# A selective state-space decoder layer on one core: state matmuls ahead of the transposes, out-projection three slots behind, parameters in a buffer of their own

## The chip, the core and the metric

The kernel runs on one core of a Trainium2 chip. The metric is the device time of one execution in microseconds (us); smaller is better. The kernel before took 816.22 us, the median of three runs (814.41 to 816.71).

## The reference, cut to what matters

Two sequences of 256 tokens (512 tokens, 512 features) go through three layers: a Mamba-2 style layer, a product with a quantised context, and a small feed-forward layer with a low-rank mixture. Nearly all time goes to the first:

```
h     = rmsnorm(layernorm(x)) * norm_w
gate, hidden, B, C, dt = split(h @ in_proj_w.T)       # 8192, 8192, 1024, 1024, 128
hidden, B, C = silu(causal_conv4(hidden, B, C))
M     = (C B^T) * exp(segment sums of A*dt)            # per head, lower triangle
y     = M @ (hidden * dt) + D * hidden
y     = groupnorm(y * silu(gate)) * gnorm_w            # 8 groups of 1024 channels
x     = x + h_in + y @ out_proj_w.T
```

There are 128 heads of 64 channels. The kernel takes two heads (128 channels) at a time, a *pair*: 64 pairs, 8 in each of 8 groups. B and C, and the norm of y, belong to a group.

## The kernel before, in words

Work is written out by hand for each engine, in program order, with semaphores between them. Every engine runs the same loop of 64 *slots* (`slots`, L200 to 209): slot s, with k = s mod 8 its place in group g. The first and the last group are written out, the six between are a hardware loop. Matrix weights and activations are split into an upper and a lower part (`_hi`, `_lo`), so a projection is three passes of four matmuls of 128x128 by 512 columns (`project`, L1093): 12 matmuls.

- **TensorE, slot s** (`@block.tensor`, `slot`): `project` of the hidden channels of pair s into `ps_h`; `scan_heads` (L1183), 8 matmuls issued as 16, which multiply the masked decay matrix of pair s-1 by its `hid_dt` into `ps_y`; at k = 0 the products of B and C (L1141, L1142) into `ps_z` and `ps_t`, at k = 1 the channel sums of the group before (L1204) into `ps_t`; `project` of the gates into `ps_z`; `project_out` (L1196, 12 matmuls) of pair s-2 into `ps_out`, which collects a group; the four transposes of `hidT` of pair s into `ps_t` (L1066). At k = 6 and 7 the projections of B and of C of the next group follow, into `ps_z`.
- **VectorE**: `hid_dt` from `ps_t` (L835, pair s-1), at k = 2 the four additions of the finished group to `acc` (`add_group`, L876), the convolution of pair s in three steps (`conv`, L728), `v` and `yg` (`combine`, L846 and L852, pair s-1), the masking of the decay of pair s (L792), `y_lo` (L858).
- **ScalarE**: the first tap of the convolution (`tap`, L477), `hidT` (L539), the gate (L545), `y_hi` and `sq` (`finish_y`, L561 and L567, pair s-1), and the 8 exponentials of the decay of pair s+1 (`decays`, L531). It loads a function table before the exponentials and another before `hidT`.
- **GpSimd**, for pair s+1: copies of its own sums (L329), split of the input weights (L288), split of the output weights (L292), lower part of the input weights (L297), the triangle of `csx` (L337), lower part of the output weights (L302); at k = 4 the split of the B and C weights (L379, L307); then the sum of squares (L399). At k = 1 it also takes the root for the group's norm (L385). It starts a slot when `project_out` of pair s-3 is done.
- **SyncE's queue**, for pair s: the row of weights and parameters (L237, after `y_lo` of pair s-4), two loads of `csx` (L245, after `decays` of pair s-2), at k = 1 the B and C weights of the next group (L259, after the Silu of the present C).

Buffers: `w_raw` and the output weights have 4 places; input weights, `csx`, `decay`, `hidT`, `gate`, `yg`, `sq` have 2; `ps_h`, `ps_z`, `ps_y`, `ps_t` one PSUM bank each.

The wait between the transposes and `scan_heads` of the next slot is what sets the order around the change:

```
eng.wait_ge(dve_hiddt, s)      # scan_heads of slot s, pair s-1
eng.wait_ge(dve_m, s)
```

## Time and profile before

| what | value |
|---|---|
| median of 3 runs | 816.22 us |
| the profiled execution | 814.25 us |
| its span, first to last instruction | 812.4 us |
| mean granted TensorE clock | 0.996 |
| TensorE busy | 787.0 us (97%) |
| VectorE, ScalarE, GpSimd busy | 615.7, 603.5, 624.1 us |
| moved by DMA | 94.93 MB, mean 117 GB/s |

The 1.85 us between span and time lie ahead of the first and behind the last instruction. The end of a matmul is modelled, so neighbours overlap in the record: the pace of matmuls is read from one start to the next, and the idle time given before a matmul is a little shorter than the time lost.

### The profile page before, as it was taken

Reading aid. Unit: us, or ns where it says so; the run is one execution under the profiler, and the core shown is the slowest. Engines: PE = TensorE matmul, PEld = TensorE weight load, DVE = VectorE, ACT = ScalarE, POOL = GpSimd, SP = SyncE. Lnnn points to the kernel's source line nnn. Section 1 sums busy time; section 2 is a strip of 40 time slices with the busy share of each in tenths; the row PEclk is TensorE's granted clock in tenths of the full one; section 3 lists DMA queues with packets and bytes.
Section 4 is the critical chain, followed back from the end, with each engine's and each line's share of the span. In section 5 each row is a group of like instructions: output and inputs, shape, how many; then the busy total and the mean of one; then the engine's idle time right before and its main releaser. Section 6 shows DMA issues by size and latency. Waiting matters only on the chain.

```text
span 812.4 us, 13296 instructions
## 1 busy us (share of the span) xinstructions
PE 787.0 (97%) x4322; PEld 607.8 (75%) x4322; DVE 615.7 (76%) x752; ACT 603.5 (74%) x1052; POOL 624.1 (77%) x552
## 2 busy tenths in 40 slices
PE   8798999999999999999999999999999999999897
PEld 7576777777777777777777777777777777777664
DVE  6889978786776867786776867776786867798864
ACT  5788777877788776877688886878688876888442
POOL 6689985799578985799578985799578986798231
PEclk9999999999999999999999999999999999999999
DMA  8452425333243324334233424333233424340001
GB/s 332 146 142 86 130 67 177 122 118 130 92 134 123 129 65 158 127 129 129 91 129 129 129 65 156 129 129 129 91 129 129 129 66 157 130 126 30 4 2 52
DMA packets 48812, 94.93 MB, mean 117 GB/s; under 512 B 3952, under 2 KB 36848, under 8 KB 48784
## 3 DMA queue, kind: packets, MB, share of 16 engines
q1 hardware_dynamic: 48496, 94.06, 35.0%
q10 hardware_dynamic: 288, 0.52, 0.2%
q8 instruction: 15, 0.25, 0.1%
q14 instruction: 13, 0.11, 0.0%
HBM read 93.26 MB, written 1.31 MB: 116 GB/s over the span
## 4 chain that ended last, share of the span: by engine, by line
PE 58%; DVE 21%; ACT 11%; issue 8%; POOL 1%; DMA 0%; ACTq 0%; DVEq 0%
PE ps_z L1093 17%; PE ps_out L1196 14%; PE ps_h L1093 12%; PE ps_y L1183 6%; DVE conv L728 5%; DVE conv_bc L728 4%; ACT decay L531 4%; DVE yg L852 2%; PE ps_t L1066 2%; ACT L531 2%; DVE v L846 2%; ACT conv L477 2%; DVE y_lo L858 2%; DVE decay L792 1%; ACT conv_bc L461 1%
## 5 line engine op out<-in xcount | busy, mean ns | idle before, releaser
L728 DVE SCALAR_TENSOR_TENSOR conv<-ps_h,w_raw,conv 128x510 f32<-128x510 f32 (+2 forms) x192 | 143.2, 746 | 94.5 <-ACT conv L477 90.0
L531 ACT ACTIVATE decay<-csx,cs_own 128x256 f32<-128x256 f32 (+1 forms) x512 | 184.4, 443 | 1.0
L297 POOL TENSOR_TENSOR win_lo<-w_raw,win_hi 128x1024 fp32r<-128x1024 f32 x64 | 153.4, 2397 | 0.5 <-DMA csx<-cs_rows 0.5
L399 POOL TENSOR_TENSOR sqacc<-sqacc,sq 128x512 f32<-128x512 f32 x47 | 70.3, 1496 | 94.1 <-ACT sq L567 94.1
L792 DVE TENSOR_TENSOR decay<-decay,cbm 128x1536 f32<-128x1536 f32 x64 | 126.0, 1968 | 2.4 <-ACT decay L531 2.4
L539 ACT ACTIVATE hidT<-conv 128x512 f32<-128x512 f32 x64 | 40.5, 634 | 94.8 <-DVE conv L728 94.8
L1183 PE MATMUL ps_y<-decay,hid_dt 128*64 128x256 f32 (+1 forms) x1024 | 97.5, 333 | 9.4 <-DVE hid_dt L835 9.4
L337 POOL TENSOR_SCALAR_AFFINE_SELECT csx<-csx 128x512 f32<-128x512 f32 x128 | 105.8, 851 | 0.2 <-DMA csx<-cs_rows 0.2
L1183 PEld LDWEIGHTS ps_y<-decay,hid_dt 128*64 128x64 f32 x1024 | 63.4, 136 | 51.9 <-issue 17.3
L1196 PE MATMUL ps_out<-wout_hi,y_lo 128*128 128x512 f32 x252 | 99.9, 397 | 0.0
L1196 PE MATMUL ps_out<-wout_lo,y_hi 128*128 128x512 f32 x252 | 99.5, 395 | 0.0
L1196 PE MATMUL ps_out<-wout_hi,y_hi 128*128 128x512 f32 x252 | 99.4, 395 | 0.0
L302 POOL TENSOR_TENSOR wout_lo<-w_raw,wout_hi 128x512 fp32r<-128x512 f32 x64 | 94.1, 1470 | 0.1
L858 DVE SCALAR_TENSOR_TENSOR y_lo<-yg,w_raw,y_hi 128x512 fp32r<-128x512 f32 x64 | 92.7, 1448 | 1.6 <-ACT y_hi L561 1.6
L531 ACT ACT_TABLE_LOAD x63 | 80.8, 1283 | 1.2
L1093 PE MATMUL ps_z<-hT_hi,win_hi 128*128 128x512 f32 x256 | 77.1, 423 | 0.5 <-DVE conv_bc L728 0.3
L1093 PE MATMUL ps_h<-hT_hi,win_hi 128*128 128x512 f32 x256 | 73.5, 408 | 0.0
L1093 PE MATMUL ps_z<-hT_lo,win_hi 128*128 128x512 f32 x256 | 70.6, 397 | 0.0
L1093 PE MATMUL ps_h<-hT_lo,win_hi 128*128 128x512 f32 x256 | 70.2, 396 | 0.0
L1093 PE MATMUL ps_z<-hT_hi,win_lo 128*128 128x512 f32 x256 | 69.9, 394 | 0.0
L1093 PE MATMUL ps_h<-hT_hi,win_lo 128*128 128x512 f32 x256 | 69.3, 392 | 0.0
L288 POOL TENSOR_SCALAR win_hi<-w_raw 128x1024 fp32r<-128x1024 f32 x63 | 65.7, 1043 | 0.0
(316 smaller groups left out, 1483.0 us busy)
## 6 DMA issues: line engine op xcount, KB each, us to landing
w_raw<-in_wmain SPq DMA_DIRECT2D x64, 772.0 KB, 4.3
csx<-cs_rows SPq DMA_DIRECT2D x128, 256.0 KB, 3.5
bc_raw<-in_wbc SPq DMA_DIRECT2D x8, 517.0 KB, 3.5
ctx_raw<-in_ctx SPq DMA_DIRECT2D x1, 2048.0 KB, 16.4
bc_raw<-in_wffn SPq DMA_DIRECT2D x2, 512.0 KB, 4.0
out_x<-acc SPq DMA_DIRECT2D x4, 256.0 KB, 2.1
acc<-in_x ACTq DMA_DIRECT2D x2, 256.0 KB, 3.7
acc<-in_x SPq DMA_DIRECT2D x2, 256.0 KB, 3.5
```

The costliest lines, as they stand in the source:

```text
L288: eng.tensor_scalar(win_hi[:, r2, :], w_raw[:, r4, 0:W_IN], 1.0, 0.0, ALU.mult, ALU.add).then_inc(hi_win, 1)
L297: eng.tensor_tensor(win_lo[:, r2, :], w_raw[:, r4, 0:W_IN], win_hi[:, r2, :].bitcast(f32), ALU.subtract).then_inc(low_win, 1)
L302: eng.tensor_tensor(wout_lo[:, r4, :], w_raw[:, r4, W_IN:W_ALL], wout_hi[:, r4, :].bitcast(f32), ALU.subtract).then_inc(low_wout, 1)
L337: eng.affine_select(out=blocks[:, :, to:to + P], in_=blocks[:, :, at:at + P], compare_op=ALU.is_ge, fill=never, base=0, pattern=[[0, 2 * B ...
L399: eng.tensor_tensor(sqacc[:], sqacc[:], sq[:, (k - 1) % 2, :], ALU.add).then_inc(pool_sq, 1)
L531: done = eng.activation(decay[:, r2, b, h, lo:lo + n], csx[:, r2, b, h, lo:lo + n], ACT.Exp, bias=cs_own[:, r2, t, h:h + 1])
L728: eng.scalar_tensor_tensor(out=out_b[:, :, back:], in0=src_b[:, :, 0:S - back], scalar=w[:, TAPS - 1 - back:TAPS - back], in1=out_b[:, :, ...
L792: eng.tensor_tensor(decay[:, r2], decay[:, r2], cbm[:].unsqueeze(2).broadcast_to([P, B, 2, MJ]), ALU.mult).then_inc(dve_m, 1)
L858: eng.scalar_tensor_tensor(out=y_lo[:, q2, :], in0=yg[:, q2, :], scalar=w_raw[:, q4, W_ALL + 6:W_ALL + 7], in1=y_hi[:, q2, :].bitcast(f32) ...
L1093: last = mm(out, w[:, k * P:(k + 1) * P], h[:, k, :], start=n == 0, stop=n == 3 * KT - 1)
L1183: done = mm(ps_y[h * HD:(h + 1) * HD, (b + 1) * S - n:(b + 1) * S], hid_dt[:, q2, src, h * HD:(h + 1) * HD], decay[:, q2, b, h, lo:lo + n] ...
L1196: done = mm(ps_out[:, t, :], y[:, q2, t * P:(t + 1) * P], w[:, q4, :], start=pair == 0 and n == 0, stop=pair == PPG - 1 and n == 2)
```

## The change

1. TensorE's slot runs hidden projection, gate projection, `project_out`, `scan_heads`, transposes. In slots k = 0 and k = 7 `project_out` stands ahead of the gate projection. The products of B and C (k = 0) use `ps_h` in place of `ps_z` and stand ahead of `scan_heads`, and the channel sums move to k = 2.
2. `project_out` takes pair s-3; two of them follow the loop. `combine`, `finish_y` and `lower_y` take pair s-2, the masking pair s-1, `decays` pair s at the start of ScalarE's slot.
3. VectorE's slot runs `combine`, `hid_dt`, additions (k = 3), masking, convolutions, `y_lo`.
4. The eight parameters of a channel leave `w_raw` for `par`, eight places of their own, loaded by a DMA of their own (64 DMAs of 4 KB), so `w_raw` is freed by the lower output weights. 
5. GpSimd starts a slot when the gate projection of pair s-1 is done, splits the output weights of pair s, not s+1, at its slot's end, and does the B and C weights last. `sq` has three places.
6. The load of B and C weights is issued at k = 3.

```diff
@@ SyncE
+                    if late(s - 7):
+                        eng.wait_ge(dve_ylo, s - 7)
+                    eng.dma_start(par[:, k, :], wpar_d[s]).then_inc(w_in[r], 16)
                     if late(s - 3):
-                        eng.wait_ge(dve_ylo, s - 3)
+                        eng.wait_ge(low_wout, s - 3)
                     eng.dma_start(w_raw[:, r, :], wmain_d[s]).then_inc(w_in[r], 16)
...
-                if k == 1:
+                if k == 3:
                     eng.wait_ge(act_bc, 2 * g + 2)
@@ GpSimd slot
-                    eng.wait_ge(w_in[n4], 16 * (2 * g + (k + 1) // 4 + 1))
-                    if first and 0 < k < 3:
+                    eng.wait_ge(w_in[n4], 32 * (2 * g + (k + 1) // 4 + 1))
+                    if late(s):
                         eng.wait_ge(pe_gate, s)
-                    if late(s - 2):
-                        eng.wait_ge(pe_out, s - 2)
...
                     split_in(n4, (k + 1) % 2)
-                    split_out(n4)
                     eng.wait_ge(csx_in[1 - r2], 32 * (4 * g + (k + 1) // 2 + 1))
                     lower_in(n4, (k + 1) % 2, s + 2)
                     select(1 - r2)
-                    lower_out(n4, s + 2)
+                if late(s - 3):
+                    eng.wait_ge(pe_out, s - 3)
+                if k == 3 and not first:
+                    eng.wait_ge(dve_ms, g)
+                    eng.tensor_tensor(rstd[:], ms[:], half_neg[:], ALU.pow).then_inc(pool_rstd, 1)
+                sum_squares(s, g, k, first)
+                split_out(r4)
+                lower_out(r4, s + 1)
                 if k == 4:
                     eng.tensor_scalar(wbc_hi[:], bc_raw[:, 0:BC_W], 1.0, 0.0, ALU.mult, ALU.add).then_inc(hi_wbc, 1)
                     lower_bc(g + 2)
@@ ScalarE slot, its new order (the first two slots have no finish_y)
+                decays(s, k)
+                if k == PPG - 1 and not last:
+                    tap_bc(0, g + 1, ps_z, conv_bc[:])
                 if k == 0:
                     tap_bc(1, g, ps_z, conv_bc[:])
...
+                tap(s, g, k)
+                finish_y(s, g, k, first)
...
                 hidden(s, k)
                 gates(s, k)
-                finish_y(s, g, k, first)
-                if not (last and k == PPG - 1):
-                    decays(s + 1, k + 1)
@@ VectorE slot
+                if not (first and k < 2):
+                    combine(s, k)
                 if not (first and k == 0):
                     scale_hidden(s, k)
...
-                if k == 2 and not first:
+                if k == 3 and not first:
                     add_group(g - 1)
+                if not (first and k == 0):
+                    mask(s, g, k)
                 if k == PPG - 1 and not last:
                     conv_group(0, g + 1, ps_z, conv_bc[:])
...
+                conv_hidden(s, k)
+                if not (first and k < 2):
+                    lower_y(s, k)
@@ TensorE slot
+                turned = k == 0 or k == PPG - 1 and not last
                 eng.wait_ge(low_win, s + 1)
                 if late(3 * s):
                     eng.wait_ge(dve_conv, 3 * s)
+                if k == 1:
+                    eng.wait_ge(dve_cb, 2 * g + 1)
                 project(ps_h[:], win_hi[:, r2, 0:KT * P], win_lo[:, r2, 0:KT * P], pe_hid)
                 if first and k == 0:
                     start_up()
+                if turned and not (first and k == 0):
+                    project_out(s, g, k)
+                if late(s):
+                    eng.wait_ge(act_gate, s)
...
+                project(ps_z[:], win_hi[:, r2, KT * P:], win_lo[:, r2, KT * P:], pe_gate)
+                if not turned and not (first and k < 3):
+                    project_out(s, g, k)
+                if k == 0:
+                    products_of_bc(s, g)
+                if k == 2 and not first:
+                    sum_channels(s, g - 1)
                 if not (first and k == 0):
                     scan_heads(s, k)
...
                 for t in range(TT):
                     done = tr(ps_t[:, t * P:(t + 1) * P], hidT[:, r2, t * P:(t + 1) * P])
...
             def project_out(s, g, k):
-                pair, q2, q4 = (k - 2) % PPG, (k - 2) % 2, (k - 2) % 4
-                eng.wait_ge(dve_ylo, s - 1)
+                pair, q2, q4 = (k - 3) % PPG, (k - 3) % 2, (k - 3) % 4
+                eng.wait_ge(dve_ylo, s - 2)
...
             slots(eng, slot)
+            project_out(PAIRS, GROUPS, 0)
             scan_heads(PAIRS, 0)
-            project_out(PAIRS, GROUPS, 0)
+            eng.wait_ge(low_wout, PAIRS - 1)
+            project_out(PAIRS + 1, GROUPS, 1)
```

## Rows read from the trace of the kernel before

**Rows 1.** The page: busy time of each engine and its share.

```profile
PE 787.0 (97%) x4322; PEld 607.8 (75%) x4322; DVE 615.7 (76%) x752; ACT 603.5 (74%) x1052; POOL 624.1 (77%) x552
```

**Rows 2.** Waits of TensorE, whole span: us in total, times, longest.

```profile
PE ps_y L1183 <- DVE hid_dt L835: 9.4, 13, 2.5
```

**Rows 3.** Busy time in stretches: length, PE, PEld, DVE, ACT, POOL, clock, DMA.

```profile
31.64:65.11 33.47, 30.32 (x160) 23.03 (x158) 27.19 (x36) 28.84 (x56) 26.20 (x22) 0.95 0.44 124
65.11:128.36 63.25, 59.64 (x315) 46.14 (x314) 55.90 (x58) 48.62 (x85) 52.36 (x43) 1.00 0.34 113
334.44:344.89 10.45, 10.45 (x60) 8.06 (x57) 6.70 (x8) 8.58 (x16) 8.25 (x9) 1.00 0.37 126
355.34:366.18 10.84, 10.52 (x60) 8.08 (x58) 10.06 (x9) 8.56 (x16) 10.84 (x8) 1.00 0.36 121
344.89:404.75 59.86, 59.48 (x316) 46.13 (x314) 44.26 (x48) 44.62 (x80) 49.73 (x43) 1.00 0.36 119
723.99:734.99 11.00, 10.51 (x59) 8.07 (x58) 10.76 (x11) 7.55 (x16) 11.00 (x9) 1.00 0.47 167
```

**Rows 4.** The timeline of TensorE in a plain slot (start, us, instructions).

```profile
337.38 1.52 PE L1183 MATMUL ps_y<-decay,hid_dt 128*64 128x256 f32 x16
338.84 1.19 PE L1093 MATMUL ps_z<-hT_hi,win_hi 128*128 128x512 f32 x4
339.86 1.10 PE L1093 MATMUL ps_z<-hT_lo,win_hi 128*128 128x512 f32 x4
340.80 1.09 PE L1093 MATMUL ps_z<-hT_hi,win_lo 128*128 128x512 f32 x4
...
344.54 0.60 PE L1066 MATMUL ps_t<-ident,hidT 128*128 128x128 f32 x4
344.89 0.48 PE L1093 MATMUL ps_h<-hT_hi,win_hi 128*128 128x512 f32 x1
```

**Rows 5.** The same for k = 1, where the channel sums follow the state matmuls.

```profile
317.02 1.05 PE L1204 MATMUL ps_t<-ones,sqacc 128*128 128x1 f32 x8
317.94 0.71 PE L1093 MATMUL ps_z<-hT_hi,win_hi 128*128 128x512 f32 x2
```

**Rows 6.** The timeline of VectorE: the plain slot, then k = 4, 5 and 2.

```profile
342.11 1.75 DVE L792 TENSOR_TENSOR decay<-decay,cbm 128x1536 f32<-128x1536 f32 x1
343.77 0.74 DVE L858 SCALAR_TENSOR_TENSOR y_lo<-yg,w_raw,y_hi 128x512 fp32r<-128x512 f32 x1
...
444.77 2.59 DVE L792 TENSOR_TENSOR decay<-decay,cbm 128x1536 f32<-128x1536 f32 x1
447.28 2.88 DVE L858 SCALAR_TENSOR_TENSOR y_lo<-yg,w_raw,y_hi 128x512 fp32r<-128x512 f32 x1
...
451.34 2.31 DVE L728 SCALAR_TENSOR_TENSOR conv<-ps_h,w_raw,conv 128x510 f32<-128x510 f32 x3 [0.58 <-ACT conv L477]
...
454.44 1.50 DVE L852 TENSOR_TENSOR yg<-v,gate 128x512 f32<-128x512 f32 x1
...
417.11 2.72 DVE L876 SCALAR_TENSOR_TENSOR acc<-ps_out,rstd,acc 128x512 f32<-128x512 f32 x4
```

**Rows 7.** The timeline of GpSimd at k = 4 and 5.

```profile
445.83 3.78 POOL L307 TENSOR_TENSOR wbc_lo<-bc_raw,wbc_hi 128x1024 fp32r<-128x1024 f32 x1
...
453.00 2.39 POOL L297 TENSOR_TENSOR win_lo<-w_raw,win_hi 128x1024 fp32r<-128x1024 f32 x1
```

**Rows 8.** The timeline of ScalarE: a plain slot, then the first group's second slot.

```profile
334.52 2.88 ACT L531 ACTIVATE decay<-csx,cs_own 128x256 f32<-128x256 f32 x8
...
43.21 0.60 ACT L545 ACTIVATE gate<-ps_z 128x512 f32<-128x512 f32 x1 [2.30 <-PE ps_z L1093]
```

**Rows 9.** The timeline of TensorE behind the last slot.

```profile
755.65 0.60 PE L1066 MATMUL ps_t<-ident,hidT 128*128 128x128 f32 x4
757.75 1.52 PE L1183 MATMUL ps_y<-decay,hid_dt 128*64 128x256 f32 x16 [1.50 <-DVE hid_dt L835]
```

**Rows 10.** DMA issues: KB each, median us to landing.

```profile
csx<-cs_rows SPq DMA_DIRECT2D x128, 256.0 KB, 3.5
```

More of the change, by code:

```diff
@@ L19 @@
 N_PAR = 8
-W_ROW = W_ALL + N_PAR
 BC_W = 2 * KT * P
@@ L499, in slot @@
                     decays(s, k)
-                    tap(s + 1, g, k + 1)
-                    decays(s + 1, k + 1)
                     return
+                if first and k == 1:
+                    tap(s, g, k)
+                    decays(s, k)
+                    scale_context(0)
+                    hidden(s, k)
+                    gates(s, k)
+                    return
+                decays(s, k)
+                if k == PPG - 1 and not last:
+                    tap_bc(0, g + 1, ps_z, conv_bc[:])
                 if k == 0:
                     tap_bc(1, g, ps_z, conv_bc[:])
-                    silu_bc(1, g, conv_bc[:])
-                if k == PPG - 1 and not last:
-                    tap_bc(0, g + 1, ps_z, conv_bc[:])
-                    silu_bc(0, g + 1, conv_bc[:])
-                if not (first and k == 1):
-                    tap(s, g, k)
+                tap(s, g, k)
+                finish_y(s, g, k, first)
                 if first:
@@ L514, in slot @@
                     scale_context(PPG - 1)
+                if k == PPG - 1 and not last:
+                    silu_bc(0, g + 1, conv_bc[:])
+                if k == 0:
+                    silu_bc(1, g, conv_bc[:])
                 hidden(s, k)
                 gates(s, k)
-                finish_y(s, g, k, first)
-                if not (last and k == PPG - 1):
-                    decays(s + 1, k + 1)
             def decays(s, k):
@@ L1159, in slot @@
                     eng.wait_ge(dve_cb, 2 * g + 2)
-                if k == 1 and not first:
+                if k == 2 and not first:
                     eng.wait_ge(dve_ms, g)
```

194 lines of the change are left out of this document (94 added, 100 removed).

## The prediction

> **What bounds the kernel now.** I read four views, in this order. The page's busy times put TensorE at 787.0 of 812.4 us [rows 1], so at most some 25 us of plain idle time are to be had by order alone. The waits of TensorE then say that nearly all of what can be named in the loop is one wait: the state matmuls wait for `hid_dt`, 9.4 us in 13 waits [rows 2]. The busy times by stretch show where [rows 3]: a plain slot of the hardware loop lasts 10.45 us and TensorE is busy in all of it, while VectorE has 6.70, ScalarE 8.58 and GpSimd 8.25 us of work. The slot k = 5 lasts 10.84 us. Five slots (k = 4 to the next k = 0) take 59.86 us in the loop, but 63.25 us in the first group. Last, the engines' timelines say what each block costs and what its neighbours are. So the kernel is bound by TensorE's own stream, and the change can give back only waits; no matmul goes away.
>
> **Why the wait exists.** Transposes of pair s-1 close a slot, `hid_dt` follows on VectorE, and the state matmuls come only one hidden projection (12 matmuls, 2.9 us) later. Where VectorE is late, TensorE waits. In the new order the gate projection (2.8 us), `project_out` (2.8 us) and the state matmuls' own turn lie between: 12 matmuls at the pace of 0.94 us for four [rows 4] are 2.8 us, so `hid_dt` and the mask have 8.4 us from the slot's start, not 2.9.
>
> **The sum, against the profiled execution's 814.25 us** (span 812.4).
>
> 1. *Loop, k = 5.* At k = 4 GpSimd has the B and C weights as well and holds up the next slot: 10.84 against 10.45, 0.39 us, in six groups 2.3 us; in the last group 11.00 against 10.45 [rows 3], 0.6 us. In all **-2.9 us**. The new cover: the weights of pair s+1 are split from the gate projection of pair s-1 on, about 4.7 us ahead of slot s, and are needed at its end, 10 us later. B and C cost GpSimd some 3.5 us (the 2.39 us of their shape [rows 7] and about 1.1 for the upper part), so all of it is hidden.
> 2. *First group from its k = 4 on.* 63.25 - 59.86 = 3.4 us above the loop's pace [rows 3], which itself holds the 0.39 us of k = 5: 3.8 us of waits. VectorE is busy 55.90 of the 63.25 us there, since it quantises the context too. That load stays; the slack grows. I take 2.8 of the 3.8 back: **-2.8 us**.
> 3. *Start.* From the second slot to k = 4 takes 33.47 us [rows 3] for three blocks of `project_out`; the new kernel does two in it and owes one (2.8 us) to the end. In the second slot the gate had waited 2.30 us for its projection [rows 8], which now stands right behind the hidden one. I followed the new order by hand with the durations of rows 4, 6 and 8: transposes of the second slot about 41 us, the third slot bound by ScalarE (a table load, 2.88 us of exponentials, the tap, two more, the context's scaling, a table load, `hidT`), k = 4 starting about 61.2 us in place of 65.11. That is 3.9 less 2.8: **-1.1 us**. B and C wait about 1 us longer in the first slot (the convolution of the hidden channels now stands ahead of that of C); this is in the 61.2.
> 4. *End.* Behind the last slot the state matmuls started 2.10 us after the transposes began [rows 9], which themselves take 0.35 us [rows 4]. The `project_out` that is now there (2.8 us) fills these 1.75 us: **-1.7 us**.
> 5. *Changing between blocks.* The state matmuls use weights of 64 columns, all others 128. The step into them keeps a 128-column neighbour before it, so it costs the same. Out of them the gate projection's first four matmuls took 1.02 us against 0.94 for the next four [rows 4]; that goes, since the gate projection follows the hidden one. The transposes follow the state matmuls instead. They took 0.35 us for four [rows 4]; the channel sums, the nearest thing that follows the state matmuls with fresh 128-column weights each time, took 0.92 us for eight [rows 5], 0.115 each, so 0.46 for four. Bounds for each of some 62 slots: -0.08 (transposes at 0.35) and +0.11 (all of it, nothing saved), -5 to +7 us. I take the middle of the two rows, +0.02 each: **+1.0 us**.
> 6. *Additions of the group, k = 3.* Their 2.72 us [rows 6] now stand ahead of the mask and of the convolution of the same slot, whose `hidT` the transposes want 10.05 us after the slot's start. From the slot's start, VectorE ends `hid_dt` at about 2, the additions at 4.7 to 5.3, the mask at 6.4 to 7.2, the convolution (2.31) at 8.7 to 9.5, `hidT` at 9.4 to 10.1. Between nothing and 0.3 us late; seven times: **+1.0 us**.
> 7. *Costed at nothing.* Channel sums, now at k = 2, and B-C products only change place on TensorE; the first has the state matmuls behind it to cover the mean that the transposes wait for (0.15 us of work), the second finds B and C done some 1.5 us early. The 64 parameter loads: one more issue on SyncE's queue per slot, waiting for `y_lo` of seven slots ago; queued behind it are the weights and `csx`, and both now wait for earlier events than before. `csx` is issued after the exponentials of the slot two back and lands 3.5 us later [rows 10], about when GpSimd asks for it; if late it costs GpSimd tenths of the 2 us it idles in a slot. The B and C load at k = 3 waits for a Silu long done, 12 us ahead of its use. Cover for all: GpSimd's slack; without it 3.5 us a group.
>
> Sum: -2.9 - 2.8 - 1.1 - 1.7 + 1.0 + 1.0 = -6.5 us: 807.7 us for the execution profiled, which stands 2.0 us under the median shown. For the median: 816.2 - 6.5 = **809.7 us**.
>
> **A lock between VectorE and GpSimd.** `y_lo` took 0.74 us in the plain slot, but 2.88 us when it met GpSimd's lower part of B and C: it ended at 450.16, 0.55 us after that operation (449.61). The mask before it took 2.59 in place of 1.75 us, and GpSimd's operation 3.78 us, where one of the same shape took 2.39. `yg` took 1.50 us and ended at 455.94, 0.55 us after GpSimd's operation of 453.00 [rows 6, 7]. `v`, `conv` and `hid_dt`, with an operand in PSUM, keep their time (conv 2.31 us beside it). So `yg`, the mask and `y_lo`, and each operation of GpSimd, take turns. Work that must take turns in a slot of 10.45 us: GpSimd's 8.25 us [rows 3] less about 0.1 us at the head of each of its eight operations (its 2.39 us operation ended 2.25 us after the mask let go), 7.4 us; VectorE's 0.55 + 1.6 + 0.55, 2.7 us; together 10.1. Until now GpSimd rested while VectorE did these three, because it waited for `sq`; now it will not.
>
> The Trainium skill, "SBUF — State Buffer", its summary of ports, speaks against this change: a VectorE instruction with two SBUF inputs and a GpSimd instruction that reads SBUF share a port under an exclusive lock, and the later one blocks fully. The trace agrees (twice 0.55 us behind the end of GpSimd's operation). By this rule at its worst the time would be that of the first rival, by VectorE's 6.70 us of the plain slot alone that of the forecast.
>
> **Rivals.**
> - *The lock makes VectorE the bound (slower).* At its worst rows VectorE's slot is v and its wait 0.9, `yg` 1.50, `hid_dt` 0.7, mask 2.59, conv 2.31, `y_lo` 2.88 [rows 6], 10.9 us. It decides where this passes 10.45. In five slots a group, eight groups: 40 x 0.45 = 18 us: 809.7 + 18, less some 5 us where longer slots (k = 0, 1, 6, 7) take up the lag: about 822 us. Against it: all three must meet the longest operation in every slot, and in my schedule one does (about 10.1 us in all). Chance 0.09.
> - *The additions and the first group stay late (no change).* If the group's root is 1 us late behind the lock, k = 3 loses 1.3 us, seven times 9 us, where I have 1; and items 2 and 3 bring nothing: about 815 to 819. For it: the root shares GpSimd with everything else. Chance 0.11.
> - *The first group alone brings nothing.* Items 2 and 3 fail: TensorE's clock was at half for about 3 us after the idle stretch of the second slot (mean 0.95 in the first stretch [rows 3]), and the new third slot idles too. 813 us. Chance 0.12.
> - *Leaving the state matmuls is free.* Item 5 at its lower bound and item 6 at nothing: 802 to 803 us. Chance 0.10.
> - *My forecast*: 805 to 813 us. Chance 0.58.
>
> 0.3% is 2.4 us, about what a measurement can tell from no change. Faster by more: the forecast, the last two rivals, 0.80; within: 0.11; slower: 0.09. The range takes in all but the slow rival and the upper half of the second: 802 to 817.
>
> **What would show it.** Right: no wait for `hid_dt` in TensorE's waits; k = 5 at 10.45 us; plain slots between 10.37 and 10.56; state matmuls at the end directly behind `project_out`; VectorE's busy time per plain slot up from 6.7 to 8 or more, with idle left. Wrong: TensorE waiting for `hidT` in many slots with VectorE busy throughout (the lock); waits at k = 3 alone (the additions); a plain slot of another length with TensorE fully busy (item 5); k = 4 of the first group later than 62 us (item 3).

## The result, and the profile after

The changed kernel takes **810.8 us** in the median (807.7 to 811.8 in five executions) against 816.1 us for the kernel before (814.4 to 816.8, six executions): a ratio of 0.9925, 95% interval 0.9907 to 0.9943. A sixth execution took 1552 us and is left out; nothing here shows why. A second measurement of it, on another chip, gave 813.4 us (804.4 to 814.2) and 0.992 (0.9885 to 0.9956). The forecast was 809.7 us, range 802 to 817. So sign and size hold, and in this there is luck: of six terms of the sum two came out as forecast, one brought nothing, one had the wrong sign and lost 3.5 us, one was seven times too small, and one, also of the wrong sign, gained 9.8 us and paid for the others.

The profiled execution took 810.7 us with a span of 808.6, 3.8 us less than before. First the page's busy times, against [rows 1]:

```profile
PE 779.3 (96%) x4322; PEld 612.1 (76%) x4322; DVE 641.4 (79%) x752; ACT 595.6 (74%) x1052; POOL 687.6 (85%) x552
```

TensorE has 7.7 us less busy time for the same 4322 instructions, so part of the gain is no removed wait. VectorE has 25.7 and GpSimd 63.5 us more for the same work. Second, what TensorE waits for (us in all, times, longest):

```profile
PE ps_t L1083 <- ACT hidT L549: 12.7, 13, 2.1
PE ps_h L1193 <- ACT bcT L474: 2.1, 1, 2.1
```

The wait for `hid_dt` [rows 2] is gone, and one for `hidT`, ahead of the transposes, stands in its place. Third, the busy times by stretch, with the columns of [rows 3]: second slot to k = 4; k = 4 to the next k = 1; from the loop k = 3 and two plain slots (the second is k = 5); five slots of the loop; the last group's k = 3.

```profile
35.13:65.82 30.69, 27.07 (x147) 20.85 (x145) 23.16 (x26) 26.07 (x50) 26.44 (x24) 0.95 0.56 171
65.82:128.97 63.15, 59.24 (x315) 46.32 (x314) 58.32 (x60) 48.15 (x84) 56.62 (x43) 1.00 0.35 107
332.87:343.81 10.94, 10.40 (x60) 8.07 (x58) 9.82 (x12) 8.09 (x15) 9.76 (x9) 1.00 0.39 122
343.81:354.14 10.33, 10.33 (x59) 8.06 (x58) 8.63 (x10) 8.63 (x17) 10.16 (x8) 1.00 0.38 111
354.14:364.45 10.31, 10.31 (x59) 8.08 (x58) 9.00 (x9) 8.37 (x16) 10.14 (x9) 1.00 0.41 132
343.81:402.36 58.55, 58.55 (x316) 46.20 (x314) 49.21 (x50) 45.22 (x81) 53.27 (x43) 1.00 0.38 113
697.41:709.43 12.02, 10.47 (x59) 8.21 (x58) 10.31 (x13) 8.11 (x15) 9.69 (x10) 1.00 0.38 109
```

From the starts of the slots, the whole account of the 3.8 us:

| stretch | before | after | difference |
|---|---|---|---|
| up to the second slot | 31.64 | 35.13 | +3.49 |
| second slot to k = 4 (one `project_out` less) | 33.47 | 30.69 | -2.78 |
| k = 4 to the next k = 1, first group | 63.25 | 63.15 | -0.10 |
| six groups of the loop | 552.91 | 547.05 | -5.86 |
| k = 1 of the last group to the last state matmuls (one `project_out` more) | 76.48 | 78.01 | +1.53 |
| the rest | 54.65 | 54.57 | -0.08 |

The six loop groups slot by slot (means of six, us; k = 1 and 2 in one column, since the channel sums moved from k = 1 to k = 2, which took 11.36 and 10.46 before and 10.30 and 11.09 after):

| k | 1 and 2 | 3 | 4 | 5 | 6 | 7 | 0 |
|---|---|---|---|---|---|---|---|
| before | 21.82 | 10.45 | 10.45 | 10.84 | 13.28 | 13.22 | 12.09 |
| after | 21.39 | 11.25 | 10.33 | 10.31 | 13.19 | 13.14 | 11.58 |

Each column is shorter except k = 3. TensorE's timeline of a plain slot, against [rows 4] (start, us, instructions):

```profile
344.83 1.08 PE L1110 MATMUL ps_h<-hT_lo,win_hi 128*128 128x512 f32 x4
345.75 1.08 PE L1110 MATMUL ps_h<-hT_hi,win_lo 128*128 128x512 f32 x4
346.67 1.07 PE L1110 MATMUL ps_z<-hT_hi,win_hi 128*128 128x512 f32 x4
347.57 1.07 PE L1110 MATMUL ps_z<-hT_lo,win_hi 128*128 128x512 f32 x4
...
352.28 1.52 PE L1207 MATMUL ps_y<-decay,hid_dt 128*64 128x256 f32 x16
353.73 0.66 PE L1083 MATMUL ps_t<-ident,hidT 128*128 128x128 f32 x4
354.14 0.48 PE L1110 MATMUL ps_h<-hT_hi,win_hi 128*128 128x512 f32 x1
```

Behind the first four, which take 1.02 us, four projection matmuls take 0.90 to 0.92 us from start to start, where [rows 4] had 0.94, and the gate projection no longer begins with a slower four (1.02 there). The transposes behind the state matmuls take 0.41 us (353.73 to 354.14), 0.06 more than in [rows 4].

And k = 3, on VectorE, then `select` and the root on GpSimd:

```profile
334.48 0.68 DVE L849 TENSOR_TENSOR hid_dt<-ps_t,dt_tok 128x512 f32<-128x512 f32 x1
336.07 2.73 DVE L890 SCALAR_TENSOR_TENSOR acc<-ps_out,rstd,acc 128x512 f32<-128x512 f32 x4 [0.92 <-POOL rstd L380]
338.72 1.75 DVE L808 TENSOR_TENSOR decay<-decay,cbm 128x1536 f32<-128x1536 f32 x1
340.38 2.30 DVE L739 SCALAR_TENSOR_TENSOR conv<-ps_h,par,conv 128x510 f32<-128x510 f32 x3
```

```profile
333.38 1.67 POOL L339 TENSOR_SCALAR_AFFINE_SELECT csx<-csx 128x512 f32<-128x512 f32 x2
335.02 1.02 POOL L380 TENSOR_TENSOR rstd<-ms,half_neg 128x4 f32<-128x4 f32 x1
```

The slot starts at 332.87. The root is done at 336.04, so the additions begin 3.20 us into it, `conv` ends at 9.8 and `hidT` at 10.5, where the transposes could have begun at 10.0.

### The profile page after: what moved, and what is told of

The parts are those of the page before. It is cut to its first block, busy times and chain, and to the rows that moved or that the text cites. A ratio compares the mean times of both kernels' runs of the same rounds, so it can differ in the third digit from the quotient of the medians.

```text
span 808.6 us, 13556 instructions
## 1 busy us (share of the span) xinstructions
PE 779.3 (96%) x4322; PEld 612.1 (76%) x4322; DVE 641.4 (79%) x752; ACT 595.6 (74%) x1052; POOL 687.6 (85%) x552
## 4 chain that ended last, share of the span: by engine, by line
PE 57%; DVE 16%; POOL 10%; issue 8%; ACT 5%; DMA 3%; SPq 1%; POOLq 0%; DVEq 0%; ACTq 0%
PE ps_z L1110 17%; PE ps_out L1220 13%; PE ps_h L1110 12%; PE ps_y L1207 6%; DVE conv L739 4%; DVE decay L808 3%; POOL csx L339 3%; DMA csx<-cs_rows 3%; PE ps_t L1083 3%; POOL win_lo L301 2%; POOL sqacc L403 2%; DVE acc L890 2%; ACT decay L541 2%; DVE ctx_raw L838 1%; ACT L541 1%
## 5 line engine op out<-in xcount | busy, mean ns | idle before, releaser
L301 POOL TENSOR_TENSOR win_lo<-w_raw,win_hi 128x1024 fp32r<-128x1024 f32 x64 | 165.9, 2591 | 14.7 <-DMA csx<-cs_rows 9.8
L739 DVE SCALAR_TENSOR_TENSOR conv<-ps_h,par,conv 128x510 f32<-128x510 f32 (+2 forms) x192 | 142.9, 744 | 17.4 <-ACT conv L483 12.9
L808 DVE TENSOR_TENSOR decay<-decay,cbm 128x1536 f32<-128x1536 f32 x64 | 149.5, 2336 | 0.1
L339 POOL TENSOR_SCALAR_AFFINE_SELECT csx<-csx 128x512 f32<-128x512 f32 x128 | 115.6, 925 | 1.0 <-DMA csx<-cs_rows 0.9
L860 DVE SCALAR_TENSOR_TENSOR v<-hidT,par,ps_y 128x512 f32<-128x512 f32 x64 | 47.6, 744 | 76.6 <-PE ps_y L1207 76.6
L403 POOL TENSOR_TENSOR sqacc<-sqacc,sq 128x512 f32<-128x512 f32 x47 | 101.9, 2169 | 6.3 <-ACT sq L577 6.3
L866 DVE TENSOR_TENSOR yg<-v,gate 128x512 f32<-128x512 f32 x64 | 79.0, 1235 | 9.2 <-DVE v L860 1.8
L872 DVE SCALAR_TENSOR_TENSOR y_lo<-yg,par,y_hi 128x512 fp32r<-128x512 f32 x64 | 70.3, 1099 | 1.0 <-ACT y_hi L571 1.0
L1110 PE MATMUL ps_z<-hT_hi,win_hi 128*128 128x512 f32 x256 | 68.9, 391 | 1.0 <-DVE conv_bc L739 1.0
L483 ACT ACTIVATE conv<-ps_h,par 128x512 f32<-128x512 f32 x64 | 49.0, 766 | 27.0 <-PE ps_h L1110 27.0
```

The source lines that it names most:

```text
L301: eng.tensor_tensor(win_lo[:, r2, :], w_raw[:, r4, 0:W_IN], win_hi[:, r2, :].bitcast(f32), ALU.subtract).then_inc(low_win, 1)
L339: eng.affine_select(out=blocks[:, :, to:to + P], in_=blocks[:, :, at:at + P], compare_op=ALU.is_ge, fill=never, base=0, pattern=[[0, 2 * B ...
L403: eng.tensor_tensor(sqacc[:], sqacc[:], sq[:, n % 2, :], ALU.add).then_inc(pool_sq, 1)
L739: eng.scalar_tensor_tensor(out=out_b[:, :, back:], in0=src_b[:, :, 0:S - back], scalar=w[:, TAPS - 1 - back:TAPS - back], in1=out_b[:, :, ...
L808: eng.tensor_tensor(decay[:, q2], decay[:, q2], cbm[:].unsqueeze(2).broadcast_to([P, B, 2, MJ]), ALU.mult).then_inc(dve_m, 1)
L866: eng.tensor_tensor(yg[:, q2, :], v[:], gate[:, q2, :], ALU.mult).then_inc(dve_yg, 1)
```

## The experiments

The questions. Is k = 3 late because of the additions' place on VectorE, or because the root of the mean squares comes late on GpSimd? Did the start lose its 3.5 us by the first slot's order, in which the tap and the convolution of C stand behind those of the hidden channels? Has the cost of leaving the 64-column matmuls gone or only moved? Do VectorE and GpSimd get in each other's way? And what are the parts worth that I costed at nothing? A letter stands for a theory as the expectation that names it puts it.

**Mask ahead of the additions at k = 3.**

```
-                if k == 3 and not first:
-                    add_group(g - 1)
                 if not (first and k == 0):
                     mask(s, g, k)
+                if k == 3 and not first:
+                    add_group(g - 1)
```

> In the changed kernel the slot k = 3 of each later group lasts 10.9 to 11.4 us instead of the plain 10.3, because the group's additions wait 0.9 us for the root on GpSimd and stand ahead of mask and convolution. Theory A (order on VectorE): with the mask ahead of the additions, the mask fills the wait for the root, the convolution ends some 0.9 us sooner, k = 3 falls to 10.3 to 10.5 us in six groups, and the time falls by 4 to 6 us against the changed kernel (about 805 to 807). Theory B (the port lock makes VectorE short of time whatever the order): k = 3 stays above 10.8 us and the time within 1.5 us of the changed kernel's 810.8.

Measured: 807.0 us (801.8 to 810.4, four executions), 0.9872 of before (0.9817 to 0.9926). The interval is wide and overlaps that of the changed kernel; the slot itself decides: k = 3 still took 10.95 to 11.31 us, and TensorE still waited for `hidT` (9.9 us in 14 waits). VectorE, and GpSimd's root, at k = 3:

```profile
333.40 2.17 DVE L808 TENSOR_TENSOR decay<-decay,cbm 128x1536 f32<-128x1536 f32 x1
336.49 2.73 DVE L890 SCALAR_TENSOR_TENSOR acc<-ps_out,rstd,acc 128x512 f32<-128x512 f32 x4 [0.92 <-POOL rstd L380]
```

```profile
333.94 2.52 POOL L380 TENSOR_TENSOR rstd<-ms,half_neg 128x4 f32<-128x4 f32 x1
```

The mask runs until 335.57, the root takes 2.52 us in place of 1.02 and ends 0.89 us behind it. The mask gets its time and the root loses it, so the additions wait just as long. From the second group's k = 1 to its end this trace takes 679.0 us, that of the changed kernel 679.7. The order on VectorE is not the cause.

**The root ahead of `select` on GpSimd.**

```
                     lower_in(n4, (k + 1) % 2, s + 2)
+                    if k == 3 and not first:
+                        eng.wait_ge(pe_out, s - 3)
+                        eng.wait_ge(dve_ms, g)
+                        eng.tensor_tensor(rstd[:], ...)
                     select(1 - r2)
```

> The root for the group's norm is taken ahead of the triangle of csx on GpSimd, about 1.6 us sooner, with VectorE's order as in the changed kernel. Theory A: the additions start right behind hid_dt, 0.9 us sooner, and k = 3 falls to 10.3 to 10.5 us as in the run with the mask first; time 805 to 807. Theory B: k = 3 stays above 10.8 us. If the wait for the root is not what counts but the 2.7 us of additions, this run gains 0.9 us of 1.0 at k = 3 and leaves 0.1 to 0.3.

Measured: 806.7 us (805.6 to 806.8, four executions), 0.988 (0.9853 to 0.9907). k = 3 took 10.33 to 10.40 us in five of its seven slots, 10.57 and 10.68 in the others. The wait of the additions is down to 0.32 us:

```profile
332.08 2.72 DVE L891 SCALAR_TENSOR_TENSOR acc<-ps_out,rstd,acc 128x512 f32<-128x512 f32 x4 [0.32 <-POOL rstd L378]
```

```profile
330.57 1.48 POOL L378 TENSOR_TENSOR rstd<-ms,half_neg 128x4 f32<-128x4 f32 x1
```

The additions themselves take 2.72 us as before. So the late root, and not the time of the additions, is nearly all of what makes k = 3 wait.

**State matmuls ahead of `project_out`.**

```
-                if not turned and not (first and k < 3):
-                    project_out(s, g, k)
...
                     scan_heads(s, k)
+                if not turned and not (first and k < 3):
+                    project_out(s, g, k)
```

> State matmuls between gate projection and project_out (k = 1 to 6), transposes behind project_out as before the change. Theory C (the plain slot's 0.14 us come from what follows the state matmuls): project_out now pays what the gate projection paid before (about 0.1 us), the four transposes go back from 0.41 to 0.35 us, the gate projection keeps its 2.73 us but for the step into 64 columns (0.09): plain slot 10.3 to 10.4 us. Theory D (the pace of both projections, 0.227 instead of 0.232 us a matmul, hangs on the state matmuls not standing between them or behind them): the gate projection goes back to 2.8 and the plain slot to 10.45. Both: k = 3 grows by 1.5 to 2.5 us, since the mask ends 7.6 us after the slot's start there and the state matmuls would want it at 5.6.

Measured: 815.7 us (812.9 to 820.5, ten executions), 1.0005 (0.9982 to 1.0029). The plain slot stays at 10.34 us. Its timeline:

```profile
346.63 1.07 PE L1110 MATMUL ps_z<-hT_lo,win_hi 128*128 128x512 f32 x4
347.54 1.07 PE L1110 MATMUL ps_z<-hT_hi,win_lo 128*128 128x512 f32 x4
348.54 1.52 PE L1207 MATMUL ps_y<-decay,hid_dt 128*64 128x256 f32 x16
349.99 0.50 PE L1220 MATMUL ps_out<-wout_hi,y_hi 128*128 128x512 f32 x1
350.33 0.39 PE L1220 MATMUL ps_out<-wout_lo,y_hi 128*128 128x512 f32 x1
```

`project_out`'s first matmul now takes 0.34 us from start to start, the others 0.22 to 0.24: leaving the 64 columns costs 0.1 us there too, and the transposes are back at 0.35. So the cost of switching only moves with the state matmuls. The gate projection keeps its pace of 0.91 us for four. The loss sits at k = 2, 11.1 to 11.9 us, and at k = 3, 11.9 to 12.1 us. At k = 3 of one group the state matmuls, now 2.8 us earlier in the slot, stand idle for 1.67 us until the mask is done, and the mask stands behind additions that had waited 1.82 us for the late root. From the second group's k = 1 to the end this trace takes 689.6 us, 9.9 more than the changed kernel's. So with the root where it is, the place behind `project_out` is needed; with the earlier root this order was not tried.

**The first slot as before** (the taps of C first, its convolution ahead of that of the hidden channels, and the B-C products into the bank that this frees).

```
-            tap(0, 0, 0)
             tap_bc(1, 0, ps_y, gate[:, 1, :])
+            tap(0, 0, 0)
...
+                if k == 0 and first:
+                    conv_group(1, g, ps_y, gate[:, 1, :])
                 conv_hidden(s, k)
```

> The first slot's B-C products use ps_y again and the convolution of C stands ahead of that of the first pair, as before the change; all else as changed. The changed kernel's second slot begins at 35.1 us instead of 31.6. Theory E (the new order of the first slot makes TensorE wait 2 us for the Silu of C, and its clock falls to half for 6 us): the second slot begins at 31.5 to 33 us, time 2 to 3 us less than the changed kernel. Rival: the late start comes from the loads ahead of it (the first projection already begins 1.3 us later), and the clock falls anyway: less than 1 us gained.

Measured: 807.2 us (805.6 to 813.9, seven executions), 0.9912 (0.9877 to 0.9947). The second slot starts at 32.55 us, 2.6 earlier; the wait for `bcT` falls from 2.1 to 1.2, and the granted clock stays at 1.00 from 31 to 38 us, where the changed kernel had 0.55. What was not expected: k = 4 to the next k = 1 of the first group takes 58.5 us without a single wait. The same stretch, and VectorE in two places of it:

```profile
64.53:123.06 58.53, 58.53 (x315) 46.14 (x314) 53.37 (x57) 47.72 (x84) 57.27 (x44) 1.00 0.37 113
```

```profile
84.20 0.85 DVE L838 TENSOR_SCALAR ctx_raw<-ctx_raw 128x512 f32<-128x512 f32 x1
...
86.61 0.90 DVE L866 TENSOR_TENSOR yg<-v,gate 128x512 f32<-128x512 f32 x1
```

and in the changed kernel, with GpSimd's two beside them:

```profile
76.50 2.62 DVE L838 TENSOR_SCALAR ctx_raw<-ctx_raw 128x512 f32<-128x512 f32 x1
...
81.26 2.03 DVE L866 TENSOR_TENSOR yg<-v,gate 128x512 f32<-128x512 f32 x1
```

```profile
75.96 2.88 POOL L311 TENSOR_TENSOR wbc_lo<-bc_raw,wbc_hi 128x1024 fp32r<-128x1024 f32 x1
...
80.34 2.40 POOL L301 TENSOR_TENSOR win_lo<-w_raw,win_hi 128x1024 fp32r<-128x1024 f32 x1
```

The same instructions in the same order cost VectorE 53.4 us there and 58.3 us here. The two long ones here end 0.28 and 0.55 us behind GpSimd's operation, so how they fall against GpSimd's decides. The start sets that, but not by the slot's order alone. Eight traces have the changed kernel's first slot, each with the wait of 2.0 to 2.1 us. In four of them (the changed kernel twice, the mask first, the root earlier) the granted clock then fell to 0.53 to 0.57 from 31 to 38 us, and the stretch from k = 4 on took 62.9 to 63.3 us. In the other four (the next three experiments and the state matmuls first) the clock stayed at 1.00, and the stretch took 59.0 to 60.0 us, except where the weight row came late (62.9, with a wait of 2.6 us of its own). In the three us before, TensorE had been busy for 0.90 to 1.09 us in both kinds. With the old first slot the clock stayed up there in each of five traces. So the order costs 0.9 us by its wait (14.24 for 13.37 us of first slot) and another 1.1 to 1.5 us where the clock falls; the 3 to 4 us of the first group went with the fall in each trace, but no experiment changes the clock alone. By k = 1 of the second group this trace is 5.9 us ahead of the changed kernel's, while the median gained 3.6, in part since this kernel's k = 3 still waited (up to 12.3 us).

**The weight row waits for `y_lo` of three slots ago, as before**, in place of GpSimd's lower part.

```
-                        eng.wait_ge(low_wout, s - 3)
+                        eng.wait_ge(dve_ylo, s - 3)
```

> The load of a weight row waits for y_lo of four pairs ago again, as before the change (the place of the parameters stays apart, so only the wait is undone). y_lo now comes a slot later in the loop than before, so the row is issued some 8 us after the start of the slot two back and lands 6 us later. Theory F (the parameters' own places are what lets the deeper pipeline run): GpSimd waits for the row, from the middle of the slot before, and starts 8 us late; its 8 us of work then end at or behind the start of the slot that needs them, and plain slots grow above 10.31 us, by up to 1 us. Rival G (GpSimd's slack covers it): plain slots stay at 10.31 us, k = 3 and k = 4 at most grow, and the time is that of the changed kernel within 3 us.

Measured, one execution: 863.9 us. The largest of TensorE's waits, and of GpSimd's:

```profile
PE ps_h L1110 <- POOL win_lo L301: 17.3, 8, 3.4
```

```profile
POOL cs_own L331 <- DMA w_raw<-in_wmain: 88.4, 33, 11.4
```

Since `y_lo` now lags a slot more, its event lets the next row go too late: GpSimd stands for the row 33 times, and k = 2, 3, 5 and 6 grow to 14.3, 12.8, 12.4 and 13.7 us in the mean of six groups; k = 1 and 4 stay at 10.3 us. With this wait the change would have been slower by 48 us than the kernel before.

**The load of B and C back at k = 1.**

```
-                if k == 3:
+                if k == 1:
                     eng.wait_ge(act_bc, 2 * g + 2)
```

> The B and C weights are loaded at k = 1 again, all else as changed. My sum costed the move at nothing: time within 2 us of the changed kernel's, no slot of another length. Rival: at k = 1 the queue waits for the Silu of C with the next row and csx behind it, GpSimd's csx comes late, and a slot k = 1 or 2 grows.

Measured, one execution: 839.8 us. The wait of the DMA queue before this load; GpSimd at k = 1 of one group:

```profile
SPq L263 <- ACT bcT L474: 107.9, 7, 17.7
```

```profile
318.56 0.73 POOL L331 COPY cs_own<-cs_tok 128x8 f32 x1 [8.87 <-DMA w_raw<-in_wmain]
```

In the new order the Silu of C comes late in ScalarE's slot. At k = 1 SyncE stands in front of the B and C load until then, 107.9 us in seven waits, and the next row and `csx` stand behind it in the queue. The changed kernel's queue has no such wait. So the new place of this load is worth 29 us, by single executions.

This trace has the changed kernel's start and all its sums, its clock stayed at 1.00 there, and its first group from k = 4 on is:

```profile
62.86:122.66 59.80, 59.23 (x316) 46.20 (x314) 53.61 (x57) 47.72 (x84) 56.58 (x43) 1.00 0.30 91
```

**Sum of squares on 8 of 512 tokens.** GpSimd's additions into `sqacc` leave out 504 of 512 columns, so the normalisation is not computed; the time tells what GpSimd's share of the lock costs.

```
-                    eng.tensor_tensor(sqacc[:], sqacc[:], sq[:, n % 2, :], ALU.add)
+                    eng.tensor_tensor(sqacc[:, 0:8], sqacc[:, 0:8], sq[:, n % 2, 0:8], ALU.add)
```

> The sum of squares takes 8 of 512 columns in all but the first of a group's additions (so the norm's sums are left out for most tokens): GpSimd loses some 1.2 us of work and of the port in 6 of 8 slots, nothing else changes. Theory H (in the first group and at k = 3 it is the shared port that makes VectorE late): the five slots from k = 4 of the first group, 63.2 us in the changed kernel, fall to 60 or less, and k = 3 of later groups falls only a little (its sum is the one in the slots before), 10.7 to 11.3. Rival: VectorE's own work sets the first group, and it stays at 62.5 to 63.5.

Measured, one execution: 798.5 us. The first group from k = 4 on:

```profile
62.69:121.67 58.98, 58.73 (x316) 46.25 (x314) 53.33 (x57) 47.72 (x84) 53.70 (x46) 1.00 0.37 114
```

Against the changed kernel VectorE's busy time falls by 5 us without any change to its work, and the stretch by 4.2. But the run before this one had 53.61 us and 59.80 us with all sums computed: this trace too is one whose clock stayed up in the first slot. So of the stretch the sums account for some 0.8 us, and the stated threshold of 60 us cannot tell the theory from its rival. At k = 3 the cut does tell: 10.33 to 10.80 us, where the changed kernel had 10.94 to 12.02 and the one with the old first slot 10.93 to 12.33. GpSimd's load has its part in that loss; for the first group it is not shown.

**Earlier root and old first slot together** (the edits of the second and the fourth experiment).

> The root taken ahead of the triangle, together with the first slot as before the change. The single runs gave spans of 804.8 and 804.7 us for 808.6: k = 3 lost 0.5 to 1.1 us six times, the first slot 2.5 us. If they add, the span is 800 to 802 us and the time 802 to 804 us, ratio to the kernel before 0.982 to 0.986. Rival: the phase in which VectorE and GpSimd meet at the port after the first slot decides what the first group costs (58.5 to 63.2 us in the runs so far), and the gain is anything from 3 to 9 us against the changed kernel, with a spread of several us between executions.

Measured: 799.3 us (797.6 to 803.7, five executions), **0.98** (0.9778 to 0.9823); k = 4 starts at 62.39 us, the stretch after it takes 59.8 us, and k = 3 takes 10.33 to 10.81.

The three next ran on one chip: the same kernel again, one more with TensorE's idle time in the start filled, and the changed kernel.

> The kernel with the earlier root and the first slot's old order, unchanged, on the same chip as the one with the filled idle time, so that 1.5 us between them can be told: again about 799 us (0.98 of the kernel before).

Measured: 801.2 us (799.4 to 803.7), 0.982 (0.9797 to 0.9843).

> The earlier root and the first slot's old order together (799.3 us), and in addition matmuls whose result nobody reads: 14 small ones behind the first gate projection, 20 behind the state matmuls of the second and third slot, in the time in which TensorE waits for hidT there. Theory I (TensorE's idle time lets its clock fall): in the kernel with the two edits the granted clock is 0.79 from 42 to 50 us, right after TensorE had been busy for 1.89 of the 4 us before; the hidden projection of that slot takes 4.4 us in place of 2.8. With the idle time filled it should stay at 1.00, the projection take 2.8 us, and the start be 1.5 us shorter: about 797.8 us. Rival J: the next slot is bound by ScalarE anyway, so the faster projection only waits longer for hidT (1.41 us there now): no change, 799.3 us, with the wait before the next transposes up by what the projection gained. Rival K: the extra matmuls come between hidT and its transposes and cost up to 0.5 us each time: 800 us or more.

```
                 project(ps_z[:], ...)
+                if first and k == 0:
+                    for _ in range(14):
+                        mm(ps_t[:, 0:P], onesb[:], onesb[:], start=True, stop=True)
...
                     scan_heads(s, k)
+                if first and 0 < k < 3:
+                    for _ in range(20):
+                        mm(ps_t[:, 0:P], onesb[:], onesb[:], start=True, stop=True)
```

Measured: 800.8 us (798.7 to 804.4), 0.9814 (0.979 to 0.9838): the same. The stretches from 38 and from 42 us without the filling matmuls (length, TensorE, clock, DMA), and then with them:

```profile
38.00:42.00 4.00, 1.88 (x19) 1.00 0.51 134
42.00:50.00 8.00, 8.00 (x36) 0.79 0.58 211
```

```profile
38.00:42.00 4.00, 3.11 (x39) 1.00 0.64 140
42.00:50.00 8.00, 7.92 (x49) 1.00 0.69 207
```

The clock stays at its upper level, 2.4 GHz, and the hidden projection takes 2.85 us (42.64 to 45.49) in place of 4.44. Yet the slot lasts 10.73 us in both: TensorE only stands longer for `hidT`. Rival J holds: a faster TensorE is worth nothing where ScalarE sets the slot. That the filling kept the clock up is not shown by this one trace: the last experiment's, without it, was busy for 1.89 of the 4 us before 42 too and had 1.00 behind them.

> The changed kernel itself, on the same chip as the two others. It gave 810.8 us (0.9925 of before) where the kernel with the mask ahead of the additions gave 807.0 on another chip, though in both k = 3 waits. If the chip and the phase of the start decide such differences, this gives between 806 and 811 us; if the mask's place is worth 4 us, it gives 811 again.

Measured: 813.4 us, above both values that were expected, and spread: three executions at 804.4 to 807.7, four at 813.4 to 814.2. Its profiled execution took 814.2 us, 3.5 more than the first one, and up to the last pair the two differ by 0.4 us. The rest of this pair is in the tail. First the execution of 810.7 us, then that of 814.2:

```profile
770.00:780.00 10.00, 10.00 (x94) 1.00 0.01 2
```

```profile
760.00:770.00 10.00, 7.89 (x58) 0.94 0.03 8
770.00:780.00 10.00, 9.84 (x61) 0.72 0.00 0
```

The clock fell behind a stretch in which TensorE was busy for 7.89 of 10 us, with two waits of 0.9 and 1.2 us in it. In the first execution it was busy for 7.96 of the same 10 us and the clock stayed at 1.00, so these waits alone do not decide it. None of its executions at 804 to 808 us was traced; that the clock stayed up in their start would fit, and is not shown. The last experiment fills these two, on top of the earlier root and the old first slot.

```
+            keep_up(ps_z, 13)
             eng.wait_ge(c_sum, 2)
-            keep_up(spare, WARM_UP // 2)
+            keep_up(spare, WARM_UP // 2 + 15)
```

> The earlier root and the first slot's old order, and behind the last pair 28 more small matmuls whose result nobody reads, 13 ahead of the wait of 0.9 us and 15 in that of 1.2 us, about 28 us before which the loop ends. Theory L (the spread of one kernel's executions, about 4 us, is the clock falling after these two waits): in the profile of the kernel with the two edits that took 799.0 us the granted clock was 0.87 from 760 to 770 us, in the one that took 795.6 us it was 1.00 there; the changed kernel had 0.72 from 770 to 780 us in an execution of 812.2 us and 1.00 in one of 808.6. With the waits filled the clock should stay at 1.00 from 750 to 780 us, the executions stay together near the fast ones (797.6 to 799.5 us), and the highest of them under 801.5. Rival M: the clock falls all the same, now or somewhere else, and the executions spread from 797 to 804 us as before. Rival N: the extra matmuls lie on the path and cost some 0.5 us each time: lowest value over 798.5 us.

Measured: 799.2 us (797.9 to 800.9, five executions), **0.9786** (0.9768 to 0.9805). Its tail:

```profile
750.00:760.00 10.00, 9.52 (x95) 1.00 0.01 4
760.00:770.00 10.00, 10.00 (x94) 1.00 0.01 2
```

The executions span 3.0 us in place of 6.0 and 4.3, all below 801. This agrees with theory L, from five executions on another chip; without the filling the clock stayed up in that tail in two of three traces with this start. A shorter median is not shown, since the intervals overlap. It is the best version found, 2.1% under the kernel before and, by the ratios, 1.4% under the changed one.

## Why the prediction was right, and where not

The total came within 1.1 us of the forecast by luck: the errors of the terms cancel. Term by term, from the tables above (us, profiled execution against profiled execution):

| term | forecast | measured |
|---|---|---|
| 1. k = 5 | -2.9 | -2.9 |
| 2. first group from k = 4 | -2.8 | -0.1 |
| 3. start, with the `project_out` owed to the end | -1.1 | +3.5 |
| 4. end | -1.7 | -1.7 |
| 5. changing between blocks, and all that remains | +1.0 | -9.8 |
| 6. additions at k = 3 | +1.0 | +7.3 |
| the rest | 0 | -0.1 |
| sum | -6.5 | -3.8 |

The median fell by 5.3 us, from 816.1 to 810.8.

**1. k = 5: right.** The slot is at 10.31 us in the loop, with no wait, for 10.84 before.

**2. First group: nothing in place of 2.8.** The step that failed is "That load stays; the slack grows". The load did not stay: VectorE's busy time there rose from 55.90 [rows 3] to 58.32 us, and k = 4 and 7 took 11.24 and 14.35 us where the kernel before took 10.68 and 13.57. In the traces whose clock stayed up in the first slot VectorE had 51.7 to 53.6 us, and the stretch took 58.5 to 60.0 but for the one with the late row; there the 60.4 that the forecast comes to was met. My estimate of VectorE by its own work was the mistake: what its operations cost beside GpSimd's differs by 5 us between traces of the same five slots. Why the clock's fall in the start and the slow first group go together is argued, not tested.

**3. Start: +3.5 where I had -1.1.** k = 4 started 0.7 us later than before (65.82 for 65.11) where I had it 3.9 us earlier (61.2), and 2.8 us are owed to the end in both. The failed step is the schedule followed, with every matmul at full clock. The wait for the Silu of C became 2.07 us for 1.1, the "about 1 us longer" of the forecast. Behind it the granted clock was 0.55 from 31 to 38 us, at its lower level of 1.2 GHz for most of that, and the products, transposes and the first eight projection matmuls took up to twice their time. With the old first slot and the earlier root the same wait was 1.2 us and the clock stayed at 1.00 there. TensorE's rows and the stretch:

```profile
31.16 0.79 PE L1193 MATMUL ps_h<-bcT 128*128 128x256 f32 x2 [2.07 <-ACT bcT L474]
...
35.13 2.06 PE L1110 MATMUL ps_h<-hT_hi,win_hi 128*128 128x512 f32 x4
```

```profile
31.00:38.00 7.00, 6.10 (x19) 4.99 (x20) 4.41 (x15) 5.26 (x12) 3.34 (x5) 0.55 0.03 11
```

Of the 4.6 us between 65.8 and 61.2, 1.35 lie ahead of all this (first projection at 19.62 for 18.27; it varied between 18.4 and 19.3 in the other kernels' traces and belongs to no edit that I tested), and 1.1 in the first slot beyond the 1 us that I had. The other 2.1 are in the three slots behind, for which the schedule leaves 28.6 us. They took 30.69, and 30.0 to 30.6 in the four traces with the same first slot whose clock stayed up in it, so the schedule was too short in itself. With the old first slot k = 4 started at 64.5, with the root moved as well at 62.4; the root's edit touches no slot of the first group, so the 2.1 us between these two are a difference between executions.

**4. End: right.** The state matmuls follow `project_out` without idle time:

```profile
753.71 0.39 PE L1220 MATMUL ps_out<-wout_hi,y_lo 128*128 128x512 f32 x1
754.03 1.52 PE L1207 MATMUL ps_y<-decay,hid_dt 128*64 128x256 f32 x16
```

The last slot, to these state matmuls, took 13.29 us for 12.20 with 2.8 us more work: 1.7 us gained. That the last group's stretch still grew by 1.5 us is this `project_out` and its k = 3 (12.02 us).

**5. Changing between blocks: -1.5 us a group where I had +0.2.** In all it is -9.8 us, outside the stated bounds of -5 to +7, and a plain slot at 10.31 to 10.33 us outside the 10.37 to 10.56 given as a sign. The step that failed took the pace of matmuls as fixed and counted the neighbours of the state matmuls alone. From the table by slot: 0.96 us a group gained, of which k = 5 gave 0.39 and k = 3 took 0.94, leaving 1.5. I had netted the transposes (+0.06, inside my bounds) against a gain of the gate projection that I bounded by its exit, 0.08 to 0.1 us. The term missing altogether was the pace of the matmuls: 0.225 to 0.230 us each in place of 0.235 in the plain slot, some 0.15 us in 24. With the state matmuls ahead of `project_out` the pace stayed, so it doesn't hang on what lies between the gate projection and `project_out`; that the two projections now stand together is what both orders share. It is not the whole of it: at k = 7 of the changed kernel `project_out` stands between them, and four still took 0.91 to 0.93 us, but for those just ahead of the state matmuls. Why the pace differs no run settles. The rest is in k = 0 (0.51 us a group: B-C products and state matmuls take 2.86 us together, 3.15 in the old order) and in the channel sums.

**6. Additions at k = 3: 1.0 us each where I had 0 to 0.3.** The step that failed is "VectorE ends `hid_dt` at about 2, the additions at 4.7 to 5.3": it let them follow at once. `hid_dt` ends at 2.3, but they begin 3.2 us into the slot, behind a root that stands behind `select` in GpSimd's list, and end at 5.9. I had named this ("If the group's root is 1 us late behind the lock") as part of a rival, with 9 us; measured, the seven slots are 7.3 us above a plain one. The rival's other half, that items 2 and 3 bring nothing, came true as well. Its own sum was wrong: 8 us more at k = 3 and 3.9 for items 2 and 3 on 809.7 are 821.6 us, not 815 to 819. Only term 5 kept the total at the forecast.

**7. Costed at nothing: right as made, but with no margin.** The two places on the queue are worth 29 and 53 us against 810.8. From the second group's k = 1 on that is 35.5 and 56.0 us, 5.1 and 8.0 a group: "Cover for all: GpSimd's slack; without it 3.5 us a group" was too low, since a late row delays GpSimd by up to 11.4 us, not by its own work.

**The lock.** VectorE did not become the bound: its plain slot has 8.63 to 9.00 of 10.3 us, up from 6.70 [rows 3], within the "8 or more" foreseen. The slow rival's condition was not met. Its mechanism can be seen in the long operations of the first group (term 2). The Trainium skill, "SBUF — State Buffer", section "Summary: rules for kernel authors", says of a VectorE instruction with two SBUF inputs and a GpSimd instruction that reads SBUF that the later one fully blocks. The trace agrees: the root took 2.52 us in the first experiment, begun 0.54 us behind the mask and done 0.89 us after it, and 1.02 us in the changed kernel.

## What to carry to other kernels

After a reordering, look for what comes late in the list of each helper engine and feeds a join: here the seven slots in which one small root on GpSimd came late lost 7.3 us, more than the whole change brought (5.3). Queue order and the event that lets a load go are part of the pipeline: when a stage moves by a slot, each wait that was written against its event has to be looked at again. Price operations of VectorE and GpSimd together. Test the start apart from the loop, and before a gain in one stretch is put down to an edit, look for the same stretch in the traces of kernels that do not have the edit: here that took away most of what the cut of the sums seemed to show. And when a total agrees, add up the terms: here two errors of 4.6 and 6.3 us and one of 2.7 stood against one of 10.8.

## What the runs showed of the hardware

- Projection matmuls of one shape take 0.225 to 0.230 us each in the plain slot where both projections stand together, and 0.235 where the state matmuls lie between them. The cause was not found.
- Behind one wait of 2.0 to 2.1 us in the first slot the granted clock fell to 0.53 to 0.57 over 7 us in four traces of eight and stayed at 1.00 in the other four.
- Five later slots with the same instructions kept VectorE busy for 58.1 to 58.5 us in the four traces with that fall, and for 53.6 us in one without it, by how its operations meet those of GpSimd.
- Over a group of executions the time goes with the clock: with a mean granted clock of 0.990 over the span the kernel before took 817.1 to 817.8 us, with 0.999 it took 814.2 to 814.5. In the one pair of traces compared, the fall that makes the difference lies in the tail. With twenty-eight small matmuls in two waits there, the best version's executions lay within 3.0 us, for 6.0 and 4.3 without them.
